# A state-space layer beside a mixture of sixteen experts: experts counted by signs, and the first tiles' work put in another order

## The reference, cut to what matters

```
xn = layernorm(x)
out = x + state_space(xn) + experts(xn)

state_space: proj = xn @ W_in -> z, x, B, C, dt, A, trap, angles
  theta = cumsum(angles * dt)                # turns, along the sequence
  K = rope(rmsnorm(B) + B_bias, theta);  Q = rope(rmsnorm(C) + C_bias, theta)
  y = causal decayed (Q K^T) x + carried state;  y = (y + D x) * silu(z);  y @ W_out
experts: top 2 of 16 by xn @ Wr + br, softmax of the two as weights
  h = silu(xn W1[e]) * (xn W3[e]);  y = layernorm(h W2[e]) * gamma[e] + beta[e]
```

## Time and profile before

| | us |
|---|---|
| median of three runs | 277.36 |
| lowest and highest | 276.57, 281.23 |
| profiled execution | 276.62 |
| its span, first to last instruction | 274.8 |
| busy in the span: TensorE, VectorE, GpSimd, ScalarE | 246.5, 226.1, 209.4, 149.3 |

### The profile page before, as it was taken

How to read it: one execution, slowest core, us unless ns; L and a number is a source line. 1 busy time by engine, 2 the same in 40 slices (tenths; PEclk the granted TensorE clock), 3 DMA queues, 4 the chain that set the end, 5 groups by cost and what they waited for, 6 DMA issues and landing times.

```text
span 274.8 us, 7393 instructions
## 1 busy us (share of the span) xinstructions
PE 246.5 (90%) x2158; PEld 219.3 (80%) x2158; DVE 226.1 (82%) x607; ACT 149.3 (54%) x508; POOL 209.4 (76%) x291
## 2 busy tenths in 40 slices
PE   2999997499999999999999999999999999999500
PEld 0857964498998999899989988998999899889400
DVE  4768998989888969896989789798969896986445
ACT  1765989646366363745364654547363755462033
POOL 8658997868798889878897989798788976665400
PEclk9999999799999999999999999999999999999965
DMA  5550837977869988897899897988978987870096
GB/s 161 173 151 8 271 119 218 291 205 197 259 208 265 290 256 253 258 279 227 260 284 248 253 250 216 296 261 249 304 236 255 288 258 242 220 248 20 23 280 177
DMA packets 68855, 61.55 MB, mean 224 GB/s; under 512 B 6608, under 2 KB 52304, under 8 KB 68816
## 3 DMA queue, kind: packets, MB, share of 16 engines
q1 hardware_dynamic: 66256, 55.83, 68.2%
q0 software_dynamic: 2560, 5.25, 6.8%
HBM read 56.27 MB, written 4.78 MB: 222 GB/s over the span
## 4 chain that ended last, share of the span: by engine, by line
PE 64%; POOL 5%; issue 4%; DVE 3%; DMA 3%; SPq 1%; ACT 1%; POOLq 0%; ACTq 0%; DVEq 0%
PE bank L876 18%; PE bank L921 10%; PE bank L819 5%; PE bank L871 5%; PE bank L811 4%; PE bank L835 3%; PE bank L766 2%; PE bank L853 2%; PE bank L844 2%; PE bank L771 2%; PE bank L796 2%; PE bank L803 2%; DMA decay<-res_dram 2%; PE bank L917 2%; POOL blk L583 2%
## 5 line engine op out<-in xcount | busy, mean ns | idle before, releaser
L876 PE MATMUL bank<-blkT,w_up 128*128 128x128 f32 x512 | 64.2, 279 | 0.6 <-ACT blkT L1090 0.4
L876 PEld LDWEIGHTS bank<-blkT,w_up 128*128 128x128 f32 x512 | 61.1, 195 | 1.3 <-issue 1.0
L637 POOL DMA_INDIRECT res_dram<-xrow,sidx x40 | 40.7, 1017 | 23.3 <-DVE xrow L1422 18.9
L583 POOL DMA_INDIRECT blk<-xn_dram,gidx x40 | 42.5, 1062 | 8.7 <-issue 7.6
L921 PE MATMUL bank<-w,xrow 128*128 128x128 f32 x256 | 34.7, 278 | 0.3 <-DVE xrow L1409 0.3
L921 PEld LDWEIGHTS bank<-w,xrow 128*128 128x128 f32 x256 | 31.1, 192 | 1.6 <-issue 1.6
L1096 ACT ACTIVATE xrow<-bank 128x512 f32<-128x512 f32 x40 | 24.5, 613 | 14.0 <-PE bank L876 13.7
L1326 DVE SCALAR_TENSOR_TENSOR kq<-sd,rms,bias_kq 128x512 f32<-128x512 f32 x32 | 22.7, 751 | 6.2 <-issue 4.8
L1394 DVE TENSOR_TENSOR xrow<-xrow,bank 128x512 f32<-128x512 f32 x40 | 27.2, 680 | 0.6 <-PE bank L876 0.6
L1090 ACT ACTIVATE blkT<-bank 128x128 f32<-128x128 f32 x40 | 11.6, 290 | 24.5 <-PE bank L862 24.4
L630 POOL TENSOR_TENSOR rstd<-mv,mhalf 128x1 f32<-128x1 f32 x40 | 24.5, 612 | 0.3
(11 more groups left out here) (246 smaller groups left out, 626.4 us busy)
## 6 DMA issues: line engine op xcount, KB each, us to landing
w_up<-in_L_ffn_W_dram SPq DMA_DIRECT2D x96, 256.0 KB
w<-in_L_ffn_W_dram SPq DMA_DIRECT2D x48, 256.0 KB
e_row<-e_dram SPq DMA_DIRECT2D x16, 256.0 KB, 4.0
decay<-l_dram SPq DMA_DIRECT2D x4, 512.0 KB, 5.6
gam<-in_L_ffn_gamma_dram SPq DMA_DIRECT2D x32, 64.0 KB
shift_y<-in_L_ffn_beta_dram SPq DMA_DIRECT2D x32, 64.0 KB
...
```

The source lines that it names most:

```text
L583: g.indirect_dma_start(out=blk[:, b % SLOTS, :], out_offset=None, in_=xn_dram, in_offset=bass.IndirectOffsetOnAxis(ap=gidx[:, entry(b):ent ...
L637: g.indirect_dma_start(out=res_dram, in_=res[:, b % HALF, :], in_offset=None, out_offset=bass.IndirectOffsetOnAxis(ap=sidx[:, entry(b):ent ...
L876: last = m(bank[out][:, c * P:(c + 1) * P], w_up[:, u % SETS, n, c * P:(c + 1) * P], blkT[:, b % 2, :], start=True, stop=True)
```

## The change

**Counting.** `pick_experts` is gone. An entry's expert is half the sum of the signs of (entry - end) over the experts, shifted by a constant: ScalarE makes two passes with `Sign` and an accumulated sum, GpSimd four small operations, and the factor of one half is in the copy to `blk_e`, which is now made within `one_hots(0)`. The transpose of the counts stands between the fourth and the fifth `sum_decays`. New waits: ScalarE's for `ends_ready`, GpSimd's for `counted`. The products of the turns are made for two tiles at a time.

```diff
-            for t in range(NT):
-                last = g.tensor_tensor(turns[:, t, :].rearrange("p (h n) -> p h n", n=NA),
-                                       bc(nar[:, t, 3 * NH:3 * NH + NA], NH, 0), bc(dtp[:, t, :], NA, 1), ALU.mult)
-                if t % TB == TB - 1:
+            pool.wait_ge(counted, 1)
+            g.tensor_scalar(behind[0:NU], full_n[0:NU], NE - 0.5, -2.0 * NE, ALU.is_gt, ALU.mult)
+            link(g.tensor_tensor(full_n[0:NU], full_n[0:NU], mix_n[0:NU], ALU.add))
+            link(g.tensor_tensor(full_n[0:NU], full_n[0:NU], behind[0:NU], ALU.add))
+            g.tensor_scalar(full_n[0:NU], full_n[0:NU], 2.0 * NE, 2.0 * (NE - 1), ALU.add, ALU.min)\
+                .then_inc(expert_ready, 1)
+
+
+            for t in range(0, NT, 2):
+                last = g.tensor_tensor(turns[:, t:t + 2, :].rearrange("p t (h n) -> p t h n", n=NA),
+                                       bc(nar[:, t:t + 2, 3 * NH:3 * NH + NA], NH, 1), bc(dtp[:, t:t + 2, :], NA, 2),
+                                       ALU.mult)
+                if t % TB == TB - 2:
                     last.then_inc(turns_ready, 1)
 
 
...
+                if t == SUMMED // 2:
+                    pe.wait_ge(expert_ready, 1)
+                    pe.wait_ge(omb_ready, 1)
+                    nc.tensor.transpose(bank[3][0:1, 0:NU], full_n[0:NU], ident[0:NU, 0:NU]).then_inc(expert_psum, 1)
                 sum_decays(t)
             sum_turns(0)
...
+
+            act.wait_ge(ends_ready, 1)
+            a(cmp_f[0:NU], ends[0:NU], ACT.Sign, scale=-1.0, bias=at_full[0:NU, 0:1], accum_out=full_n[0:NU, 0:1])
+            a(cmp_m[0:NU], ends_l[0:NU], ACT.Sign, scale=-1.0, bias=from_mix[0:NU, 0:1], accum_out=mix_n[0:NU, 0:1])\
+                .then_inc(counted, 1)
             act.wait_ge(lrow_ready, 1)
             a(erow[0:NT * NH, :], lrow[0:NT * NH, :], ACT.Exp).then_inc(erow_ready, 1)
...
+                dve.wait_ge(s["sq_done"], 2 * (t + 1))
+                again(dve, s["rms_ready"], t)
+                ts(ms[:, :], ms[:, :], 1.0 / DS, EPS, ALU.mult, ALU.add).then_inc(s["ms_ready"], 1)
+
 
             def one_hots(k):
 
                 q0, q1 = k * NT, (k + 1) * NT
                 link(tt(row_h[:, q0:q1, :], bc(iota_k, NT, 0), bc(blk_h[:, k, :], NB, 1), ALU.is_equal))
```

```diff
+
+                gather(1)
+                rms_pow(0)
+                gather(2)
+                gather(3)
+                square_own(0)
+                rot_sine(0)
+                gather(4)
+                finish(0)
+                square_own(1)
+                gather(5)
+                pool.wait_ge(sidx_ready, 1)
+
+
+            def second_tile():
+
+                rms_pow(1)
+                weigh_q(0)
+                rot_sine(1)
+                gather(6)
+                finish(1)
+                store(0)
+                gather(7)
+                square_own(2)
+                finish(2)
+                gather(8)
+                store(1)
+                weigh_q(1)
+                gather(9)
+                store(2)
+                gather(10)
+
             def iteration(t, first, second, blocks):
                 b0, b1, b2 = blocks
...
             sum_turns(1)
+            invert(1)
             sum_turns(2)
-            invert(1)
             sum_turns(3)
...
+            def begin():
+
+                pe.wait_ge(sidx_ready, 1)
+                for _ in range(WARM_BLOCKS):
+                    m(bank[6][:, :], ident[:, :], xnT[:, 0:512], start=True, stop=True)
+                turn_block(0)
+                pe.wait_ge(theta_ready, 2)
+                rise(0)
+                turn_block(1)
+                rise(1)
+                turn_block(2)
+                down(0)
+                turn_block(3)
+                turn_k(0)
+                state_product(0)
+                turn_q(0)
+
             def iteration(t, first, second, blocks):
                 b0, b1, b2 = blocks
-                begins, ends_ = t == 0, t == NT
...
+            def begin():
+
+                absolutes(0)
+                out_block(0)
+                nc.scalar.preload_act_table_set("silu_and_others")
+                act.wait_ge(rest_in, 16 * RESTS)
+                sines(0)
+                silu(0)
+                out_block(1)
+                silu(1)
+                out_block(2)
+                weigh(0)
+                move_x(0)
+                gates(0)
+                out_kq(0)
+
...
-
             one_hots(0)
-            pick_experts()
             one_hots(1)
+            mean_square(0)
 
...
+            def begin():
+
+                cut_turns(0)
+                cut_turns(1)
+                cut_turns(2)
+                dve.wait_ge(rest_in, 16 * RESTS)
+
+                dve.wait_ge(theta_psum, 1)
+                weigh_bc(0)
+                norm_kq(0)
+                cut_turns(3)
+                rot_cosine(0)
+                product(0)
+                rotate(0)
+                product(1)
+                norm_y(0)
+                diagonal(0)
+                diagonal(1)
+
             def iteration(t, first, second, blocks):
                 b0, b1, b2 = blocks
```

179 lines of the change are left out of this document (75 added, 104 removed).

## The result

The changed kernel takes 280.0 us (median of 20 runs, 277.91 to 281.61) beside 277.62 us for the kernel before on the same chip (20 runs, 276.50 to 281.23): a ratio of 1.0078, interval 1.0055 to 1.0100. That is 2.4 us more than the kernel before, where 277.0 and no change were forecast, and just over the range's 279.8. The profiled execution took 278.97 us with a span of 277.2 us (before: 276.62 and 274.8).

The account below looks back on a forecast made before the run. TensorE's pace bounds the woven loop, so only the front or waits count; 2.2 us gained there are lost because GpSimd's third norm comes 0.3 later. 276.62 plus 0.3 is 276.9, forecast 277.0, range 274.2 to 279.8.

Parts of the forecast that it names:

- The front: Up to the mixed block's pass: earlier gather and full clock keep 2.2 us of the 6.1 that can be gained.
- the place named: TensorE in front of the second half of rise(6): the 2.2 us are lost in a stall of 2 to 3 us.
- Part 2: Indices and first gather: gidx written at about 42.3, first gather at 43.9, 2.0 us earlier.
- part 4's sum: GpSimd from finish(0) to the third norm: 56.7 + 17.3 + 2.5 + 0.65 = 77.15, against 76.83, 0.3 us later.
- diagonal(0)'s wait: Wait inside GpSimd's stretch from finish(0) to the third norm, put at 0.35 us.
- work and issue: GpSimd's stretch from finish(0): 17.3 us as in the kernel before, plus 2.5 for two gathers more.
- 0.3 for norm_kq(1): GpSimd's wait for VectorE's second-tile norm, inside the stretch from finish(0) to the third norm: 0.3 us.
- rival 2: weigh_q(0) beside norm_kq(1), both reading SBUF: VectorE's norm waits up to 1.3 us, 278.2; chance 0.15.
- rival 3: Late squares(0) hold back the indices by 1.5 us: 278.5, or 279.8 with the slow pass back; chance 0.15.
- Rival 1: GpSimd keeps up, the 2.2 us stay and TensorE never stalls at rise(6): 274.4, or 273.5; chance 0.2.

Follow-up runs that it names:

- experiment 2: Changed kernel with three unused 384-column matmuls on TensorE inside the wait of rise(6), in front of its second half: 278.59 us, ratio 1.0042.
- 4: Changed kernel with ScalarE's function table load ahead of the first block's copy: 279.51 us, ratio 1.0089.
- 5: Changed kernel with GpSimd's old order of calls put back in begin and second_tile: 275.87 us, ratio 0.9914.
- 6 (without warm blocks): Changed kernel without its two unused 512-column matmuls in front of the first block: 279.17 us, ratio 1.0061.
- 8: Changed kernel, GpSimd's old order, weigh_q(0) behind rot_sine(1): 275.58 us; table load ahead too: 275.13; five gathers ahead with both edits: 276.65.
- five gathers ahead: Changed kernel with all five gathers moved ahead in GpSimd's order, weigh_q(0) and its lock left in place: 276.76 us, ratio 0.9992.
- experiment 1: Changed kernel with weigh_q(0) behind rot_sine(1) instead of in front of it on GpSimd: 279.88 us, ratio 1.0095.

## Why the prediction was wrong

**What held.** The front gave what was forecast: rise(0) at full clock, block 0 at 49.40 (forecast 48.8), product(0) at 53.29 (53.3 to 53.9), the statistics at 56.77 to 56.92 (56.7), finish(0) after a wait of 1.64 us (2.5), rise(2) at 58.95 (58.9). And the gain was lost at the place named, in a wait of TensorE at the second half of rise(6), 2.68 us (2 to 3). The step from the third norm factor to the keys held as well: 7.02 us before, and 6.98 to 7.02 in the profiles of experiments 2, 4, 5, 6 (without warm blocks), 8 and with five gathers ahead, all with the clock full behind rise(6).

Two of these hits are partly luck. Block 0 was 0.6 us late and the sines ended at 51.96 (51.6), but VectorE's second rotation product (L1416) took 0.94 us where the forecast had the 2.18 of L1344, so that product(0) was on time. And the 2.68 us belong to a norm factor 1.2 us later than forecast: with the factor at 76.87, near the forecast 77.15 (five gathers ahead), TensorE's wait at rise(6) is 0.62 us.

**Part 2 was off, and it cost little.** The indices came 1.9 us later than forecast. The compares took 2.72 us each, not 2.48 and 2.71; the small instructions ahead of them were slower, and the first one-hots began at 32.57 and not 31.68, beside GpSimd's eight turns (5.68 us, forecast 5.8) and count (1.2 us, forecast 1.4); mean_square(0) took 0.59. The first gather was 1.2 later than forecast. Block 0 made half of it good: it landed 4.3 us after its gather's start (4.9).

**The step that failed** is part 4's sum, "0.3 us later". Against its own terms: the start was 57.01 (forecast 56.7, +0.31), diagonal(0)'s wait 0.26 (0.35), work and issue 78.31 - 57.01 - 1.61 = 19.69 us (19.8), and "0.3 for norm_kq(1)" measured 1.35. This one term holds 1.05 of the 1.16 us by which 77.15 was too early. It was rival 2's lock, near the size given there (1.3). The Trainium skill ("SBUF — State Buffer", section "SBUF: two separate sides") has the rule, and the trace agrees: 2.37 us for 1.41. But rival 2 read it as a cost on top of an order that is sound without it, and experiment 1 shows that it isn't: without the lock the two operations stand one behind the other, and GpSimd loses as much. The sum had no row for the pair and took the smaller end. Its other terms hold two slips that cost little: three stores are queued there and not two (the 17.3 us have all three), and 0.79 us of these 17.3, in front of the store at 71.31 in the kernel before, were for the most part a wait for VectorE and not work.

Nor does that sum say what bounds the norm factor. Counted from finish(2), the forecast's gain is there (72.32 to 70.11 is 2.21 us earlier) and 3.69 us of queue are added behind it (8.20 less 4.51), which is the +1.48 measured. The forecast saw two gathers more in the whole list. It did not see that a store and two gathers had crossed finish(2), the last instruction in it whose data come late, from a place where GpSimd stands anyway to one where it never does.

**The missing term** is the clock. The forecast named the wait of 2 to 3 us at rise(6), put no cost on the clock behind it, and named the half clock only for the front, in rival 3. Its price behind rise(6) is 1.19 us (experiment 2). 276.62 + 1.48 + 1.19 is 279.3, against 278.97 measured for that execution; 277.0 had 0.3 for both.

**The rivals.** Rival 1 asked for the statistics sooner or the waits gone, and did not happen in the changed kernel: TensorE stalled at rise(6). What it describes, a front gain that stays, came with the old order on GpSimd, and smaller (275.87, where rival 1 had 274.4). Rival 2 happened as a lock (2.37 us for 1.41), with its 278.2 short of the 280.0. Rival 3 (squares late) did not happen: mean_square(0) started right behind the compare, with no idle time, and that its 279.8 is close to the measured 280.0 is luck.
